# An attention and feed-forward layer on one core: new due times for slot zero's statistics, additions and low parts, and for slot one's first scores

## The chip, the cores and the metric

The kernel runs on one core of a Trainium2 chip. The metric is the device time of one execution in microseconds (us): the median of the runs, less is better.

## What is computed

There are 8 slots (batches) of x and ctx, each [512, 2048] in fp32. The reference, cut to what matters:

```python
xn = layernorm(x)                                # over the 2048 columns of each row
t, p, g = Wt @ ctx, Wp @ xn, Wg @ ctx            # [512, 512] weights
att = sum over each group of 64 rows of p * g    # one number per group
y  = Wz (per group) @ (att * t)
yn = groupnorm(y) * gn_w + gn_b
x  = x + yn + ctx
h  = layernorm(x)[:, perm] as 16 heads of 128 columns
x  = x + unpermute(down[head] @ gelu(up[head] @ h))
```

## The kernel before, in words

**The algebra.** Since att is a sum of products of p and g, the kernel never forms p or g. It forms the scores S = x ctx^T over the 2048 columns (16 blocks dt of 128), corrects S with the mean and the deviation of x's rows, multiplies it by Wp (stage v_mm) and reduces it against Wg (v_att). Wz Wt is folded into one matrix at the start (fold_mm), and Y = (Wz Wt) ctx is computed in four quarters q of 512 columns (y_mm). Then come the group statistics (g_mean, g_var_mm, g_var_a, g_root, g_var_b), the sum (x1_piece), the second layernorm, a transposed store to a scratch in HBM, and the units of the feed-forward part, which gather 128 rows by an index, run up, gelu, down and scatter the result.

**High and low parts.** TensorE takes fp32 operands rounded to its fp32r format. For full accuracy each operand is split: ScalarE makes the high part (s_hi line 976, y_hi line 982), VectorE the low part by subtraction (s_lo line 1084, y_lo line 1090). TensorE runs three products: high x high (s_hh line 874, for four banks c1), then low x high and high x low (s_mm lines 879 and 880). For Y a group of twelve matmuls (line 892 x8, then line 896 x4) makes one tile ot of one quarter; the last four need the low part.

**The order of work.** There is one plan, `plan()`. Each stage gets a due time by `put(t, stage, ...)`, in units of about 2.72 us (the time of one block). The stages are sorted by due time, and each engine then runs its own stages in that one order, first in, first out. A stage waits on semaphores for its inputs and for its buffers (`take` and `give`), and an engine's later stages wait behind it. So a due time does nothing but set the order on the engines. Slot zero starts at base 0, its y0 is 16, v0 is 32 and f0 is 36; slot one starts at base 36.

**The stages around the change, in slot zero.**
- VectorE: bn_x (statistics of x tile ct, quarter q; 16 pieces, line 1069), aggr_x (line 1076), s_lo, y_lo, add_c (X += ctx, 16 pieces, line 1096, on VectorE for slot zero alone), sum_c (lines 1107 to 1112), bn_y (line 1132), s_fix (line 1120), s_evl (line 1126), v_att (line 1151), g_mean, g_var_a (lines 1171 and 1173), g_var_b.
- ScalarE: s_hi, y_hi, row_c (row sums of ctx, four pieces a quarter, line 991), y_ev (empties two banks of Y, line 998), s_evh (line 1006). In the order: y_hi(0,1), row_c(0,1,0..3), y_ev(0,0,0), row_c(0,2,0..3), y_ev(0,0,1), y_hi(0,2), row_c(0,3,0..3), y_ev(0,1,0).
- GpSimd (POOL): the splitting of the feed-forward weights, head by head: load_raw (two transfers of 256 KB), w_hi (line 1278), w_lo (line 1283), keep_w (a store of 1,024 KB, line 1288); then root_x, g_root. The stage w_hi(11) waits for s_lo(0,15) beside its data.
- SyncE: all other loads. ctx quarters c(0,q) and score blocks s(i,j) share three buffers RAW. c(0,1) takes the one of s(0,6), c(0,2) that of s(0,7), and so waits for s_lo(0,15); c(0,3) takes the one of c(0,0), and so waits for y_lo(0,0), row_c(0,0,*) and add_c(0,0,*).
- TensorE: y_mm(0,q,ot) waits for y_hi(0,q), for y_lo(0,q) ahead of its last four matmuls, and for y_ev of the quarter before for its bank. s_hh(1,0,c1) waits for v_att(0,c1), which reads the same bank. The waits of the first block and of the variance matmul, in the code:

```python
                if dt == 0:
                    for t in free["sb", i, c1]:
                        pe.wait_ge(*t)
...
            elif stage == "g_var_mm":
                i = a[0]
                pe.wait_ge(*at["gst", i, "sum"])
```

DMAs issued by GpSimd go to the queue that the profile calls q0 software_dynamic, those of SyncE to q1 hardware_dynamic.

## Time and profile before

| | |
|---|---|
| median of 3 runs | 1518.26 us |
| the runs | 1518.26, 1518.87, 1514.97 us |
| span of the profiled execution | 1516.6 us (the page gives no other time of it) |
| TensorE busy | 1496.1 us, 99% |
| VectorE, ScalarE, GpSimd busy | 1192.4, 1065.8, 962.8 us |
| mean granted TensorE clock | 0.999 |
| DMA | 374.76 MB, mean 247 GB/s |

The span goes from the first to the last instruction of one profiled execution; the times of the runs are taken without a profile. A matmul's end is modelled in the profile, so a busy share of TensorE says that it had matmuls in flight, not that none was late. Starts are exact, and some matmul records are missing. Matmuls of one group stand merged in the timeline with their count. Times in the views are us from the start of the span.

### The profile page before, as it was taken

The page shows a single profiled execution, that of the slowest core. Times are in us where ns is not written, and L with a number is a line of the kernel's source. Part 1 is how long each engine was busy: PE and PEld are TensorE (multiplying, and loading weights), DVE is VectorE, ACT ScalarE, POOL GpSimd, SP SyncE. Part 2 cuts the span into 40 slices and gives each one's busy share as a digit, 9 for nine tenths or more (in the row PEclk, how much of TensorE's full clock was granted, in tenths as well). Part 3 has the DMA queues.
Part 4 walks back from the last instruction along what each step waited for, and adds up shares of the span by engine and source line. Part 5 has one row for each costly group of instructions (what it writes and reads, how often), then busy time and mean ns, then how long its engine had stood idle before and what let it go on. Part 6 is the DMA issues. An engine that isn't in the chain of part 4 may idle for free.

```text
span 1516.6 us, 19144 instructions
## 1 busy us (share of the span) xinstructions
PE 1496.1 (99%) x6592; PEld 1233.7 (81%) x6592; DVE 1192.4 (79%) x1514; ACT 1065.8 (70%) x1321; POOL 962.8 (63%) x765
## 2 busy tenths in 40 slices
PE   8999999998999999999999999999999999999998
PEld 7878888887888888888888888888888888777886
DVE  4989868875788767887678877888778876889876
ACT  4636757844878568784687847878378773899876
POOL 1673686297862668626784357834579355898887
PEclk9999999999999999999999999999999999999999
DMA  9998788786677936778376784767747776768886
GB/s 327 330 379 332 229 301 298 269 265 204 202 264 266 276 118 221 246 262 278 119 237 248 246 260 133 261 237 250 231 146 275 249 237 204 236 197 257 289 285 221
DMA packets 166865, 374.76 MB, mean 247 GB/s; under 512 B 14960, under 2 KB 80496, under 8 KB 158576
## 3 DMA queue, kind: packets, MB, share of 16 engines
q1 hardware_dynamic: 141424, 281.25, 56.3%
q0 software_dynamic: 25344, 92.29, 17.3%
q8 instruction: 52, 0.85, 0.2%
q14 instruction: 45, 0.37, 0.1%
HBM read 287.45 MB, written 86.03 MB: 246 GB/s over the span
## 4 chain that ended last, share of the span: by engine, by line
PE 80%; DVE 4%; POOL 4%; DMA 4%; ACT 3%; issue 3%; SPq 0%; POOLq 0%; ACTq 0%; DVEq 0%
PE PP L892 13%; PE PP L938 12%; PE PP L953 12%; PE PP L896 6%; PE PP L941 6%; PE PP L957 6%; PE PP L879 6%; PE PP L880 6%; PE PP L874 6%; PE PP L909 4%; PE PP L913 2%; POOL out L1346 1%; POOL FB L1338 1%; POOL FB L1341 1%; ACT Z L1031 1%
## 5 line engine op out<-in xcount | busy, mean ns | idle before, releaser
L938 PE MATMUL PP<-GG,WW 128*128 128x512 f32 x1008 | 270.5, 390 | 4.4 <-issue 4.4
L1046 ACT ACTIVATE PP<-PP 128x1024 f32<-128x1024 f32 x256 | 262.0, 1024 | 0.0
L1249 DVE TENSOR_TENSOR R<-PP,R 128x1024 fp32r<-128x1024 f32 x175 | 213.6, 1220 | 52.5 <-ACT PP L1046 50.6
L892 PE MATMUL PP<-R,WC 128*128 128x512 f32 x1024 | 253.1, 389 | 0.7 <-ACT Z L998 0.7
L1330 POOL TENSOR_TENSOR X<-X,RAW 128x512 f32<-128x512 f32 x112 | 189.2, 1725 | 96.4 <-DVE bn L1069 71.6
L1045 ACT ACTIVATE R<-PP 128x1024 fp32r<-128x1024 f32 x175 | 180.1, 1029 | 87.5 <-PE PP L941 86.5
L938 PEld LDWEIGHTS PP<-GG,WW 128*128 128x128 f32 x1008 | 189.6, 188 | 44.4 <-issue 4.8
L892 PEld LDWEIGHTS PP<-R,WC 128*128 128x128 f32 x1024 | 192.1, 188 | 41.0 <-ACT Z L998 1.1
L1084 DVE TENSOR_TENSOR R<-RAW,R 128x1024 fp32r<-128x1024 f32 x128 | 184.1, 1445 | 49.8 <-ACT R L976 49.8
L1346 POOL DMA_INDIRECT out<-FB,perm_sb x128 | 153.4, 1198 | 82.0 <-DVE FB L1255 64.1
L1323 POOL DMA_INDIRECT FB<-xg_scratch,perm_sb x128 | 127.7, 997 | 115.1 <-DMA xg_scratch<-FB 74.4
L879 PE MATMUL PP<-R 128*128 128x512 f32 x512 | 200.5, 392 | 0.1
L880 PE MATMUL PP<-R 128*128 128x512 f32 x512 | 200.2, 391 | 0.0
L1338 POOL TENSOR_TENSOR FB<-FB,SMM 128x512 f32<-128x512 f32 x128 | 167.3, 1307 | 49.8 <-DVE GG L1244 38.3
L1341 POOL TENSOR_TENSOR FB<-FB,SMM 128x512 f32<-128x512 f32 x128 | 186.6, 1458 | 10.1
L953 PE MATMUL PP<-R,WW 128*128 128x512 f32 x688 | 185.5, 391 | 2.0 <-DMA WW<-w_scratch 2.0
L976 ACT CAST R<-RAW 128x1024 fp32r<-128x1024 f32 x128 | 132.1, 1044 | 73.2 <-PE PP L880 47.2
L941 PE MATMUL PP<-GG,WW 128*128 128x512 f32 x504 | 155.9, 391 | 0.9 <-DVE GG L1244 0.9
L874 PE MATMUL PP<-R 128*128 128x512 f32 x512 | 150.1, 392 | 5.4 <-ACT R L976 5.2
L953 PEld LDWEIGHTS PP<-R,WW 128*128 128x128 f32 x688 | 128.0, 188 | 28.6 <-issue 2.7
L1255 DVE TENSOR_TENSOR FB<-PP,FB 128x512 f32<-128x512 f32 x128 | 87.7, 685 | 64.9 <-PE PP L957 63.0
L896 PE MATMUL PP<-R,WC 128*128 128x512 f32 x512 | 137.1, 390 | 1.2 <-DVE R L1090 1.1
(122 smaller groups left out, 2582.5 us busy)
## 6 DMA issues: line engine op xcount, KB each, us to landing
WW<-w_scratch SPq DMA_DIRECT2D x148, 512.0 KB
X<-in_x SPq DMA_DIRECT2D x32, 1024.0 KB, 6.0
RAW<-in_cx SPq DMA_DIRECT2D x32, 1024.0 KB
RAW<-in_xT SPq DMA_DIRECT2D x63, 512.0 KB
RAW<-in_cT SPq DMA_DIRECT2D x63, 512.0 KB
xg_scratch<-FB SPq DMA_DIRECT2D x104, 256.0 KB
w_scratch<-WW POOLq DMA_DIRECT2D x16, 1024.0 KB, 6.8
HX<-wp_scratch SPq DMA_DIRECT2D x7, 1024.0 KB, 8.2
```

What stands on the lines that cost most here:

```text
L874: eng.matmul(s_bank(c1), hi[:, 0, part(c1)], hi[:, 1, :], start=(dt == 0), stop=False)
L879: eng.matmul(s_bank(c1), lo[:, 0, part(c1)], hi[:, 1, :], start=False, stop=False)
L880: eng.matmul(s_bank(c1), hi[:, 0, part(c1)], lo[:, 1, :], start=False, stop=(dt == ND - 1)).then_inc(S["smm"], 1)
L892: eng.matmul(PP[2 + ot // 2][:, ot % 2, :], WC[:, l, ct, part(ot)], u[:, ct, :], start=(l == 0 and ct == 0), stop=False)
L896: t = eng.matmul(PP[2 + ot // 2][:, ot % 2, :], WC[:, 0, ct, part(ot)], u[:, 4 + ct, :], start=False, stop=(ct == NT - 1))
L938: eng.matmul(pp[:, e, :], wt[:, l, part(2 * p + e)], g[:, 0, :], start=(l == 0), stop=False)
L941: t = eng.matmul(pp[:, e, :], wt[:, 0, part(2 * p + e)], g[:, 1, :], start=False, stop=True)
L953: eng.matmul(PP[1][:, f % 2, :], wt[:, 2 + l, part(2 * p + e)], hi[:, e, :], start=(p == 0 and e == 0 and l == 0), stop=False)
L1046: eng.activation(pp[:], pp[:], ACT.Gelu).then_inc(S["gelu"], 1)
L1249: eng.tensor_tensor(h_tile(f, p, 1), PP[slot["up", f, p]][:], f32(h_tile(f, p, 0)), ALU.subtract).then_inc(S["hlo"], 1)
L1330: eng.tensor_tensor(X[:, ct, cols(q)], X[:, ct, cols(q)], RAW[slot["c", i, q]][:, ct, :], ALU.add).then_inc(S["xc"], 1)
L1341: eng.tensor_tensor(rows, rows, SM[b % 2][:, 1], ALU.add).then_inc(S["radd"], 1)
```

## The change

The change gives new due times to some stages; no stage is added or removed, and no stage's code is touched. In slot zero: the statistics of x tiles 1 to 3 (bn_x) are due 0.85 later, which puts them behind s_lo(0,15) and partly behind y_lo(0,0); y_lo(0,1) is due at 15.45, not 16.6; the additions add_c have a table of their own, which puts those of quarters two and three behind y_lo(0,2). g_var_mm, g_var_a and g_root are due one block later. In slot one the first score matmul of the fourth bank, s_hh(1,0,3), is due at 36.35, not 36.24.

Sorted by due time, the orders of ScalarE, GpSimd and SyncE stay as they were. On TensorE s_hh(1,0,3) comes behind s_mm(1,0,0), and g_var_mm(0) behind the four s_hh(1,3,*) rather than behind those of block 2. VectorE's order from s_lo(0,14) on, before and after:

```
before: s_lo 14, bn_x(1,0..3), s_lo 15, bn_x(2,0), y_lo 0, bn_x(2,1..3), add_c(0,0), bn_x(3,0..1),
        add_c(0,1), bn_x(3,2..3), add_c(0,2..3), y_lo 1, add_c(1,0..2), aggr_x, add_c(1,3), bn_y(0,0..1),
        add_c(2,0..2), y_lo 2, bn_y(0,2), add_c(2,3), bn_y(0,3), add_c(3,0), sum_c, ...
after:  s_lo 14, s_lo 15, bn_x(1,0..2), y_lo 0, bn_x(1,3), bn_x(2,0..3), add_c(0,0..1), bn_x(3,0), y_lo 1,
        bn_x(3,1), add_c(0,2), bn_x(3,2..3), add_c(0,3), add_c(1,0..2), aggr_x, add_c(1,3), bn_y(0,0..1),
        y_lo 2, add_c(2,0), bn_y(0,2), add_c(2,1), bn_y(0,3), add_c(2,2), sum_c, add_c(2,3), ...
```

```diff
--- before.py
+++ after.py
@@ -602,12 +602,12 @@
             put(t + 0.2, s_lo, i, dt)
             for c1 in range(NT):
                 whole = i < 2 or dt > 3
-                put(s0 + (dt + 0.08 * c1 if whole else S_EARLY[c1 // 2][dt][c1 % 2]), s_hh, i, dt, c1)
+                put(s0 + (0.35 if (i, dt, c1) == (1, 0, NT - 1) else dt + 0.08 * c1 if whole else S_EARLY[c1 // 2][dt][c1 % 2]), s_hh, i, dt, c1)
                 put(s0 + (dt + 0.34 + 0.16 * c1 if whole else S_EARLY[c1 // 2][dt][c1 % 2]), s_mm, i, dt, c1)
         for q in range(NQ):
             for ct in range(NT):
                 t = s0 + 6 + 2.1 * ct + 0.4 * q + (1.9 if ct == 3 else 0)
-                t = 10.4 + 1.4 * ct + 0.22 * q if first else s0 + 11 + 2.1 * ct + 0.5 * q if i == 1 else t
+                t = 10.4 + 1.4 * ct + 0.22 * q + (0.85 if ct else 0) if first else s0 + 11 + 2.1 * ct + 0.5 * q if i == 1 else t
                 put(t, bn_x, i, ct, q)
         if first:
             for ct in range(NT):
@@ -619,11 +619,11 @@
         put(y0 + (12.4 if 0 < i < 3 else 4.2), load_wg, i)
         for q, t in enumerate((y0 - 3, y0 + 0.4, y0 + 4.3, y0 + 8.3)):
             put(t, y_hi, i, q)
-            put(t + 0.2, y_lo, i, q)
+            put(y0 - 0.55 if first and q == 1 else t + 0.2, y_lo, i, q)
         for q, t in enumerate((y0 - 1, y0 + 1.2, y0 + 2.6, y0 + 4.6)):
             for ct in range(NT):
                 put(t + 0.25 * ct + late, row_c, i, q, ct)
-                put(y0 - 1.5 + 2.4 * q + 0.5 * ct + 2 * late, add_c, i, q, ct)
+                put(y0 + (-1.2, 0.9, 4.6, 6.4)[q] + 0.5 * ct if first else y0 - 1.5 + 2.4 * q + 0.5 * ct + 2 * late, add_c, i, q, ct)
         put(y0 + 5.8 + late, sum_c, i)
         put(y0 + 5.9 + late, store_sum, i)
         put(y0 + 7.6 + late, spread_sum, i)
@@ -648,9 +648,9 @@
         put(v0 + 3.4, aggr_y, i)
         put(f0 + 1.2, g_mean_mm, i)
         put(f0 + 1.25, g_mean, i)
-        put(f0 + 2.3, g_var_mm, i)
-        put(f0 + 2.35, g_var_a, i)
-        put(f0 + 2.4, g_root, i)
+        put(f0 + (3.3 if first else 2.3), g_var_mm, i)
+        put(f0 + (3.35 if first else 2.35), g_var_a, i)
+        put(f0 + (3.4 if first else 2.4), g_root, i)
         put(f0 + (3.9 if first else 5.25), g_var_b, i)
```

## Rows read from the trace of the kernel before

**Rows 1.** the page: busy time, share of the span and instructions of each engine

```profile
PE 1496.1 (99%) x6592; PEld 1233.7 (81%) x6592; DVE 1192.4 (79%) x1514; ACT 1065.8 (70%) x1321; POOL 962.8 (63%) x765
```

**Rows 2.** TensorE's waits, whole span; us in total, times, longest

```profile
PE PP L938 <- issue: 4.4, 1, 4.4
```

**Rows 3.** TensorE's timeline, 52 to 82 us: start, us, engine, line, operation

```profile
52.24 1.07 PE L874 MATMUL PP<-R 128*128 128x512 f32 x4
...
53.70 0.39 PE L880 MATMUL PP<-R 128*128 128x512 f32 x1
...
66.19 1.98 PE L892 MATMUL PP<-R,WC 128*128 128x512 f32 x8
...
69.30 1.99 PE L892 MATMUL PP<-R,WC 128*128 128x512 f32 x8
...
72.03 1.98 PE L892 MATMUL PP<-R,WC 128*128 128x512 f32 x8
...
77.47 1.98 PE L892 MATMUL PP<-R,WC 128*128 128x512 f32 x8
...
81.56 1.98 PE L892 MATMUL PP<-R,WC 128*128 128x512 f32 x8
```

**Rows 4.** TensorE's timeline, 100 to 120 us

```profile
100.60 1.15 PE L909 MATMUL PP<-R,HX 128*128 128x512 f32 x4
...
111.57 0.84 PE L874 MATMUL PP<-R 128*128 128x512 f32 x3
...
112.92 0.39 PE L879 MATMUL PP<-R 128*128 128x512 f32 x1
...
117.72 1.07 PE L874 MATMUL PP<-R 128*128 128x512 f32 x4
...
119.34 0.48 PE L879 MATMUL PP<-R 128*128 128x512 f32 x1
```

**Rows 5.** VectorE's timeline, 47 to 91 us

```profile
49.72 2.47 DVE L1069 BATCH_NORM_STATS2 bn<-X 128x6 f32<-128x512 f32 x4
...
53.83 2.73 DVE L1090 TENSOR_TENSOR R<-RAW,R 128x2048 fp32r<-128x2048 f32 x1
...
65.93 2.28 DVE L1090 TENSOR_TENSOR R<-RAW,R 128x2048 fp32r<-128x2048 f32 x1
...
75.98 4.48 DVE L1090 TENSOR_TENSOR R<-RAW,R 128x2048 fp32r<-128x2048 f32 x1
```

**Rows 6.** GpSimd's timeline, 47 to 82 us; in brackets idle time before, and releaser

```profile
53.37 1.04 POOL L1278 CAST WW<-FB 128x1024 fp32r<-128x1024 f32 x1 [3.55 <-DVE R L1084]
...
59.12 0.56 POOL L1288 DMA_DIRECT2D w_scratch<-WW  x1 [0.30 <-POOL WW L1283]
...
75.60 2.72 POOL L1283 TENSOR_TENSOR WW<-FB,WW 128x1024 fp32r<-128x1024 f32 x1
```

**Rows 7.** DMA queues from 52 to 57, then 57 to 60 us: packets, MB, share

```profile
q0 software_dynamic: 278, 1.50, 73.0%
q1 hardware_dynamic: 275, 0.55, 29.3%
...
q1 hardware_dynamic: 516, 1.02, 94.0%
q0 software_dynamic: 19, 0.02, 3.1%
```

**Rows 8.** ScalarE's timeline, 47 to 100 us

```profile
47.49 2.00 ACT L976 CAST R<-RAW 128x1024 fp32r<-128x1024 f32 x2 [5.77 <-DMA RAW<-in_cT]
...
60.03 1.91 ACT L982 CAST R<-RAW 128x2048 fp32r<-128x2048 f32 x1 [5.24 <-DMA RAW<-in_cx]
...
64.74 1.00 ACT L998 COPY Z<-PP 128x1024 f32<-128x1024 f32 x1
...
71.35 0.63 ACT L991 ACTIVATE FB<-RAW 128x512 f32<-128x512 f32 x1
...
99.77 0.69 ACT L1006 ACTIVATE R<-PP,rs 128x512 fp32r<-128x512 f32 x1 [1.22 <-DVE PP L1120]
```

## The prediction

> **What bounds the kernel now.** I read the page first: TensorE is busy for 99% of the span [rows 1], so time moves only where TensorE waits, and every other engine matters by what it makes TensorE wait for. The list of TensorE's waits comes next. Its second entry, 4.4 us, is one wait near 351 us for the gathered rows of slot two [rows 2], which the diff does not name; the rest are small. The list undercounts, because a matmul's recorded end is modelled. So I read the starts in the timeline: twelve matmuls take 2.73 us from start to start, 0.227 us each (69.30 to 72.03), and a longer step is a loss [rows 3].
>
> Five losses lie beside instructions that the diff moves:
> - last scores of slot zero: 52.24 to 53.70 is 1.46 us for five matmuls (the fifth has no row here), due 1.14: **0.32 us**;
> - first Y group of quarter one: 66.19 to 69.30 is 3.11 against 2.73: **0.39 us**;
> - first Y group of quarter two: 77.47 to 81.56 is 4.09 against 2.73: **1.37 us**. These three are in [rows 3];
> - first scores of slot one: 111.57 to 112.92 is 1.35 for four, due 0.91: **0.44 us**;
> - the matmul for the group variance: 117.72 to 119.34 is 1.62; 0.91 for the four before it and about 0.2 for the two tiny ones leave **0.5 us**. These two are in [rows 4].
> Together 3.0 us, 0.2% of the time. That is all the change can win directly.
>
> **The change part by part.** Sorting the stages by their due times, old and new, shows that the order changes on VectorE and TensorE alone; the ScalarE, GpSimd and SyncE orders are the same, and nothing is added or removed.
>
> (a) s_lo(0,15) goes ahead of the four statistics of x tile 1. It ran behind bn_x x4, which began at 49.72 [rows 5]. Its source was ready: the two s_hi from 47.49 took 2.00 us, to 49.5 [rows 8]. So it now runs 49.7 to 50.9. TensorE needs it at 53.15. Gain 0.32. Price of the moved statistics: nothing, they have until aggr_x near 70.
>
> (b) y_lo(0,0) then starts at 50.9 + 3 x 0.6 = 52.7 instead of 53.83, bn_x(0,1,3) behind it. It meets GpSimd, see (c). In the trace, when GpSimd's subtraction was there first (75.60 to 78.32), y_lo took 4.48 us from 75.98 instead of 2.28, so it waited 2.2 us, to 78.2, and then ran [rows 5, 6]. GpSimd's subtraction now runs 52.1 to 54.8 at worst, y_lo(0,0) ends by 57.0; TensorE, 0.32 earlier, wants it at 55.0 + 1.8 = 56.8. Cost 0 to 0.2; I take 0, and 0.2 stays in the range.
>
> (c) What hangs on s_lo(0,15) beside TensorE: GpSimd's w_hi(11) waits for it, and in the trace it was released by it at 53.37 after 3.55 us idle [rows 6]. It now starts at 51.0, 2.4 us earlier, and its subtraction is ahead of y_lo(0,0), not behind it. So keep_w(11) and load_raw(13), issued from 59.12 on [rows 6], are issued from about 55. That is 1.57 MB (1,024 KB and two of 256 KB) on the software queue, 4 us earlier. SyncE's load_c(0,2) waits for s_lo(0,15) too and is issued 2.4 us earlier, behind load_c(0,1) on the same queue, so it gives nothing.
>
> What that traffic meets: between 52 and 57 us the software queue moved 1.50 MB and the hardware queue 0.55 MB, in 278 and 275 packets; between 57 and 60 us, with the software queue empty, the hardware queue moved 1.02 MB in 516 packets [rows 7]. So sharing costs the hardware queue two thirds of its pace (55 packets per us against 172, a factor 3.1), with the engines full in both. The context quarter c(0,1) is what it carries, and it landed at 60.0, when ScalarE, idle for 5.24 us, took it [rows 8]. In the changed kernel the software queue is not empty from 57 on: 1.57 MB at 0.30 MB per us is 5.2 us, to 62.2. If the last part of c(0,1) needs all of the 3.0 us from 57 to 60 to itself, 5.2 us shared do 1.7 us of it, and it lands at 63.5. If only 2 of the 3 us are its own, 57 + 2 x 3.1 = 63.2. Bounds: 60.0 (it is done before the traffic reaches its engines) and 65.2 (it is held for all 5.2 us). I take 63.2, by the shared pace, the only row that has both queues busy.
> The Trainium skill, "DMA: Bandwidth & Descriptors", section on queues, rings and completion order, says that each DMA engine takes its queues in turn, packet by packet. By the near-equal packet counts the trace agrees; were it instead shared by bytes, c(0,1) would land near 61.5 and the sum below would be -1.7.
>
> Who waits for c(0,1): ScalarE's order is y_hi(0,1), four row sums, then y_ev(0,0,0), which started at 64.74 and ended at 65.74 [rows 8]. That frees the bank for y_mm(0,1,0), which started at 66.19 on time [rows 3]. So TensorE can start quarter one no sooner than landing + 5.7. With TensorE 0.32 early at 65.87, any landing after 60.2 costs one for one; this slack was 0.45 us before. At 63.2 quarter one starts at 68.9, **2.7 us later** than before.
>
> (d) y_lo(0,1) goes ahead of five statistics and two additions, and starts when y_hi(0,1) ends (landing + 1.95) instead of at 65.93 [rows 5]. It is needed 1.8 us after the quarter's start, 7.5 after the landing, and ends 4.2 to 6.5 after it. Gain 0.39, kept.
>
> (e) y_lo(0,2) goes ahead of add_c(0,2,0..2). In the trace it began at 75.98, with GpSimd's subtraction from 75.60 in its way [rows 5, 6]. Now it starts at about 72.9 (landing 60.0) or 75.5 (63.2, where y_hi(0,2) and the statistics bring it) and is needed at 79.0 or 81.6. Gain 1.37, kept unless it is blocked for more than 3.8 us; the longest block seen is 2.2.
>
> (f) The additions pushed back give their buffers later: c(0,3) takes the buffer of c(0,0), which add_c(0,0,3) gives up at 65.93, just before y_lo(0,1) [rows 5]. Now that addition ends 4.2 + 3.1 = 7.3 us after c(0,1) lands, 67.3 or 70.5. c(0,3) was in ScalarE's hands at 71.35, 5.4 us after its issue [rows 8], so it comes at 72.7 or 75.9; row sums and y_ev(0,1,0) end 3.9 later, 76.6 or 79.8. TensorE wants that bank at 76.8 or 79.8. Cost 0, but with no slack.
>
> (g) First scores of slot one: the fourth bank's matmul goes behind two that wait for nothing (0.45 us), more than the wait: gain 0.44. (h) The variance matmul goes one block (2.7 us) later: gain 0.5, and x1's chain behind it starts up to 0.6 us later, hidden because nothing of TensorE's waits on slot zero's x1 pieces in this stretch; its list of waits names none.
>
> **Sum.** +2.7 - 0.39 - 1.37 - 0.44 - 0.5 = 0.0 us; for a landing L after 60.2, the net is L - 63.2. The span stays 1516.6. The page gives the span of the profiled execution alone; the median of the runs is 1.7 above it, and their own spread is 1514.97 to 1518.87. I forecast 1518.2. About 0.3% (4.6 us) is what a measurement of this kernel can tell from no change.
>
> **Rivals.**
> 1. The direct gains come through: the traffic does not slow c(0,1). For it: most of c(0,1) may be home by 57. Against: rows 7 show full engines. -3.0, so 1515.2. Chance 0.27.
> 2. TensorE is early and is stopped at v_mm. s_evh's last piece ended at 100.46 and v_mm began at 100.60 [rows 4, 8]: 0.14 us of slack on a chain that comes from sum_c through two transfers. sum_c should come 4 us earlier; if those transfers do not, 2.1 of the 3.0 us go: -1.0, so 1517.3. Chance 0.08.
> 3. Slower: c(0,1) is held for the whole burst (65.2, +2.0) and c(0,3) in its turn by the burst of keep_w(12), now issued after root_x at about 77. With no slack in (f), every us beyond 5.4 counts; the same hold costs 3.2. +5.2, so 1523.4. It decides from the point where c(0,1) lands after 63.2 or c(0,3) takes over 5.4 us. Chance 0.08.
> 4. Faster by more: the 4.4 us wait at 351 us [rows 2] hangs on a chain of stores, transposes and gathers; a shifted start may shorten it. -3 to -7, about 1513. Chance 0.10.
> 5. It does nothing that shows, each wait being taken over by its neighbour: 1518.3. Chance 0.05.
> The forecast's own chance is 0.42, its own range -1.7 to +1.5.
>
> The range, 1512.8 to 1521.8, holds the forecast, rivals 1, 2 and 5 and half of 3 and 4. Faster by over 0.3%: 0.13 (rival 4 and the edge of 1); slower: 0.05; within: 0.82.
>
> **What the changed profile would show.** Right: s_lo(0,15) before 51; w_hi(11) at 51; keep_w(11) near 55; y_hi(0,1) starting near 63 with ScalarE idle for 8 us before it; TensorE's quarter one starting near 69 behind y_ev; no step over 2.8 us at the first groups of quarters one and two; none at the first scores or the variance matmul. Wrong: y_hi(0,1) still at 60 (rival 1); a gap ahead of the first v_mm (rival 2); y_hi or row sums of c(0,3) after 76 with a gap at quarter two (rival 3); another size of the gap near 351 (rival 4).

## The result, and the profile after

The changed kernel is slower. Its median is 1525.02 us (1520.4 to 1528.72, 16 runs) against 1518.57 us (1514.81 to 1524.65, 16 runs) for the kernel before on the same chip: a ratio of 1.0038, 95% interval 1.0027 to 1.0049. That is 6.45 us more, outside the forecast range. The profiled execution took 1524.99 us with a span of 1523.2 us.

The page of the changed kernel, its span and its busy times (beside [rows 1]):

```profile
span 1523.2 us, 19144 instructions
PE 1497.9 (98%) x6592; PEld 1232.9 (81%) x6592; DVE 1194.8 (78%) x1514; ACT 1065.4 (70%) x1321; POOL 959.2 (63%) x765
```

TensorE's waits in the changed kernel (engine, line waited for: us in total, times, longest):

```profile
PE PP L892 <- ACT Z L998: 8.4, 3, 4.5
...
PE PP L909 <- ACT R L1006: 1.7, 1, 1.7
PE PP L938 <- issue: 0.6, 1, 0.6
```

The wait of 4.4 us near 351 us [rows 2] is down to 0.6. In its place TensorE waits three times, 8.4 us in all, at the first eight matmuls of a Y group (L892) for ScalarE to empty their bank (L998), near 76, 180 and 345 us; before, that was one wait of 0.7 us. TensorE's timeline shows where (start, us, engine, line, operation, count; idle time and its releaser in brackets):

```profile
65.20 1.98 PE L892 MATMUL PP<-R,WC 128*128 128x512 f32 x8
...
67.92 1.98 PE L892 MATMUL PP<-R,WC 128*128 128x512 f32 x8
...
75.18 1.07 PE L896 MATMUL PP<-R,WC 128*128 128x512 f32 x4
78.11 2.11 PE L892 MATMUL PP<-R,WC 128*128 128x512 f32 x8 [1.86 <-ACT Z L998]
...
99.09 1.07 PE L896 MATMUL PP<-R,WC 128*128 128x512 f32 x4
101.87 1.16 PE L909 MATMUL PP<-R,HX 128*128 128x512 f32 x4 [1.72 <-ACT R L1006]
...
113.77 0.39 PE L880 MATMUL PP<-R 128*128 128x512 f32 x1
114.64 0.50 PE L874 MATMUL PP<-R 128*128 128x512 f32 x1 [0.49 <-DVE am L1151]
...
178.51 1.07 PE L896 MATMUL PP<-R,WC 128*128 128x512 f32 x4
184.03 3.78 PE L892 MATMUL PP<-R,WC 128*128 128x512 f32 x8 [4.45 <-ACT Z L998]
187.61 1.74 PE L896 MATMUL PP<-R,WC 128*128 128x512 f32 x4
189.19 2.01 PE L892 MATMUL PP<-R,WC 128*128 128x512 f32 x8
```

By the pitch of 0.227 us, the changed kernel loses 2.0 us at 78.11, 1.9 at 101.87 and 0.6 at 114.64. The first Y group of quarter one (65.20 to 67.92, 2.72 us) has lost its wait, as forecast [rows 3]. **The large loss lies in slot one, ahead of quarter two of Y.** The four matmuls from 178.51 are due to be followed at 179.42; the next starts at 184.03, 4.6 us late. The eight after it take 3.58 us from start to start (184.03 to 187.61) in place of 1.81, and the four after these 1.58 in place of 0.91. That is another 2.4 us, 7.0 together. In that second part the granted clock is at its lower level. Stretches of the changed kernel (us, busy time of each engine with instructions, PEclk, DMA share, GB/s):

```profile
180.00:184.00 4.00, 0.00 (x0) 0.00 (x0) 2.39 (x4) 2.36 (x6) 3.40 (x4) 0.77 0.78 214
184.00:188.00 4.00, 3.97 (x9) 3.14 (x10) 3.88 (x7) 3.97 (x6) 3.98 (x5) 0.50 0.86 255
188.00:192.00 4.00, 4.00 (x17) 3.21 (x16) 4.00 (x5) 0.06 (x1) 4.00 (x3) 0.87 0.85 193
```

TensorE stands idle, and its granted clock falls from full speed to 0.50 (2.4 to 1.2 GHz), and the first matmuls behind the wait run at half speed.

One matmul of the group mean (L923) marks each slot. It moves from 115.44 to 117.05 in slot zero (+1.6), from 215.12 to 223.23 in slot one (+8.1), from 364.09 to 368.42 in slot two (+4.3, since the wait near 351 gives some back in this execution), and stays at +4.3 up to the last slot, 1291.36 to 1295.71. The profiled spans differ by 6.6; the other 2.3 us come behind that mark, where this stretch varies from 224.5 to 228.9 us over the profiles of this case. That remainder has no cause here.

What ScalarE's bank waited for is told by the chain of waits of the changed kernel, read from 50 to 200 us (start, us, what; "issue" is time in which the profile shows no wait):

```profile
74.10 14.15 DMA FB<-in_down
88.31 1.05 POOL WW L1278
...
115.30 8.57 DMA FB<-in_down
123.93 1.75 POOL WW L1278
...
129.38 1.06 POOL rs L1315
...
132.62 1.20 DVE Z L1206
...
154.72 8.07 ACT Z L1031 x4
...
172.58 1.31 POOL X L1330
...
173.97 7.61 DMA RAW<-in_cx
...
183.08 0.91 ACT Z L998
```

It reads: the loads of GpSimd's weight heads (in_down) are late, so g_root (L1315), which stands behind the heads on GpSimd, is late, so slot zero's x1 (L1206) is late; behind it come the second layernorm, the statistics and additions of slot one, the load of c(1,3) into the buffer they free, its row sums (L991) and the emptied bank (L998). The same stations in the kernel before, on VectorE, GpSimd, ScalarE and TensorE:

```profile
84.13 1.04 POOL L1278 CAST WW<-FB 128x1024 fp32r<-128x1024 f32 x1 [3.65 <-DMA FB<-in_down]
...
124.68 1.87 POOL L1315 TENSOR_TENSOR rs<-ve,half 128x4 f32<-128x4 f32 x1
...
128.66 1.28 DVE L1206 SCALAR_TENSOR_TENSOR Z<-Z,sm,X 128x1024 f32<-128x1024 f32 x1
...
175.31 0.64 ACT L991 ACTIVATE FB<-RAW 128x512 f32<-128x512 f32 x1 [2.38 <-DMA RAW<-in_cx]
176.70 0.99 ACT L998 COPY Z<-PP 128x1024 f32<-128x1024 f32 x1
...
178.40 1.98 PE L892 MATMUL PP<-R,WC 128*128 128x512 f32 x8
```

There the bank is emptied at 177.7 and taken at 178.40. So the chain already had only 0.7 us of slack before the change, behind no wait in any list. After it, the first x1 piece is 4.0 us later and c(1,3) 6.3.

### The profile page after: what moved, and what is told of

The parts are those of the page before. It is cut to its first block, busy times and chain, and to the rows that moved or that the text cites. A ratio compares the mean times of both kernels' runs of the same rounds, so it can differ in the third digit from the quotient of the medians.

```text
span 1523.2 us, 19144 instructions
## 1 busy us (share of the span) xinstructions
PE 1497.9 (98%) x6592; PEld 1232.9 (81%) x6592; DVE 1194.8 (78%) x1514; ACT 1065.4 (70%) x1321; POOL 959.2 (63%) x765
## 4 chain that ended last, share of the span: by engine, by line
PE 72%; POOL 9%; DMA 7%; issue 5%; ACT 4%; DVE 2%; SPq 0%; POOLq 0%; ACTq 0%; DVEq 0%
PE PP L953 12%; PE PP L938 12%; PE PP L892 11%; PE PP L941 6%; PE PP L957 6%; PE PP L896 5%; PE PP L874 5%; PE PP L879 5%; PE PP L880 5%; PE PP L909 3%; DMA FB<-in_down 3%; POOL FB L1338 2%; POOL out L1346 2%; PE PP L913 2%; POOL FB L1341 2%
## 5 line engine op out<-in xcount | busy, mean ns | idle before, releaser
L892 PE MATMUL PP<-R,WC 128*128 128x512 f32 x1024 | 255.0, 391 | 8.4 <-ACT Z L998 8.4
L892 PEld LDWEIGHTS PP<-R,WC 128*128 128x128 f32 x1024 | 193.1, 189 | 49.8 <-ACT Z L998 9.6
L1341 POOL TENSOR_TENSOR FB<-FB,SMM 128x512 f32<-128x512 f32 x128 | 189.9, 1484 | 10.1
L1255 DVE TENSOR_TENSOR FB<-PP,FB 128x512 f32<-128x512 f32 x128 | 87.6, 684 | 62.5 <-PE PP L957 62.5
```

Of the source, the lines that this page charges most:

```text
L892: eng.matmul(PP[2 + ot // 2][:, ot % 2, :], WC[:, l, ct, part(ot)], u[:, ct, :], start=(l == 0 and ct == 0), stop=False)
L1341: eng.tensor_tensor(rows, rows, SM[b % 2][:, 1], ALU.add).then_inc(S["radd"], 1)
```

## The experiments

A ratio is that to the kernel before, run beside the variants on the same chip; its medians were 1518.91, 1518.53, 1519.71, 1518.34 and 1519.63 us beside the five groups. Each variant has 12 timed runs; of the 35 runs of the kernel before beside group C one took 3913.82 us, which does not move the median. A view shows one execution, and not always a typical one: c1, c4, d1, e1 and f2 were profiled in executions 4.7 to 9.0 us above their own medians. In c1, c4, f1 and f2 TensorE starts 8.3 to 9.9 us late near 360 us, in the other profiles of this case 0.8 to 4.6 (the kernel before 4.6, the changed one 0.8). So the medians tell what a variant costs, and the views, up to the mark of slot one, where it loses. "Lost near 184" is the late start of TensorE at quarter two of slot one and what the matmuls behind it lose.

**Group A: the change taken apart.** a1 is the changed kernel with g_root (due at 39.4) put ahead of the last weight head on GpSimd; the other three are the kernel before with some lines of the shown diff.

```diff
 a1 (on the changed kernel)
         put(t, load_raw, h)
+        t += 3.1 if h == 3 else 0
         put(t + 3.3, w_hi, h)
 a2: the lines of s_hh(1,0,3), g_var_mm, g_var_a, g_root alone
 a3: the line of bn_x alone
 a4: the lines of y_lo(0,1) and add_c alone
```

> The changed kernel with one more edit: GpSimd does g_root of slot zero before it splits head 3 (w_hi, w_lo, keep_w of head 3 are due after it), not after. Theory (the loss is made on GpSimd: its weight pipeline is late, g_root stands behind it, and x1, the statistics of slot one, c(1,3) and y_ev of slot one follow): g_root ends near 125 instead of 130.4, the stalls of TensorE in quarter three of slot one (178 to 189 us in the changed kernel, 7 us in all) fall to under 1.5 us, and the time falls by 3 to 7 us, to 1518 to 1522. Rival (the loss is made in slot zero by the later c(0,3) and the sum chain, and slot one's stall has its own cause, the loads of slot one): the stall stays at 5 us or more and the time within 1.5 us of the changed kernel's 1525.

> The kernel before with the last two parts of the change alone: s_hh(1,0,3) behind s_mm(1,0,0), and g_var_mm, g_var_a, g_root of slot zero one block later. Both theories: 0.4 to 1.0 us are won at 111 to 120 us; g_root stays behind the store of head 3 on GpSimd, so nothing behind it moves by more than 0.7 us. Time 1517.6, within 1.5 us of before. Rival (the later variance matmul delays x1 and through it slot one): a stall over 2 us at quarter three of slot one, and 2 to 5 us slower.

> The kernel before with only bn_x of tiles 1 to 3 due 0.85 later: s_lo(0,15) and y_lo(0,0) come forward, y_lo(0,1) and the additions keep their due times. Theory: GpSimd's head 11 starts 2.4 us early, its store and the loads of head 13 meet c(0,2), and y_lo(0,0) waits for GpSimd's subtraction; c(0,3) is issued at 66 to 67 as before, the burst behind it does not meet the loads of head 14. Slot one has no long stall; time within 2 us of before, 1517 to 1520. Rival (the early head 11 is what makes GpSimd's pipeline late): w_hi of head 14 starts after 87, g_root ends after 129, 3 to 7 us slower.

> The kernel before with only y_lo(0,1) ahead and the new table for add_c of slot zero; the statistics keep their due times. Theory: add_c(0,0,3) ends later, so c(0,3) is issued 2 to 3 us later than 66.1, and with it the loads and stores of 3 MB that stand behind it on SyncE; they meet keep_w(12) and the loads of head 14, w_hi of head 14 starts after 87 instead of 84.1, g_root ends 3 to 5 us later, slot one stalls: 3 to 7 us slower, 1521.5 to 1525.5. Rival (the early head 11 does it): w_hi of head 14 within 1 us of before, time within 2 us of before or up to 2 us faster, since y_lo(0,2) is in time.

| | median, us | ratio (95%) | first x1 piece | lost near 184 |
|---|---|---|---|---|
| a1 | 1519.93 | 1.0013 (0.9992 to 1.0034) | 129.24 | 0.9 |
| a2 | 1518.55 | 1.0009 (0.9991 to 1.0027) | 128.54 | 1.3 |
| a3 | 1518.33 | 1.0002 (0.9988 to 1.0016) | 128.79 | none |
| a4 | 1522.14 | 1.0015 (1.0004 to 1.0025) | 130.80 | 2.6 |

a1: with g_root ahead of the last head most of the loss is gone, though the wait ahead of v_mm (1.76 us) is as long as in the changed kernel. So the chain over g_root counts, and that wait does not decide. The last head itself now runs beside VectorE's small operations behind it (one of 128x4 takes 2.25 us in place of 0.16), and x1 is still 0.6 us late. a2: TensorE's two parts do nothing that shows. The slot-zero mark is 1.0 us early (114.43) and the slot-one mark only 0.3 (214.85): the gain is swallowed where slot one is gated. a3: the statistics alone do nothing that shows either; TensorE stops 1.05 us at 65.40, since y_hi(0,1) came at 60.70. That is my step (c) in small. a4: the lines of VectorE's low parts and additions make part of the loss (1.0015 against the changed kernel's 1.0038, intervals that do not meet). But here c(0,3) was issued at 66.1, the same as in the kernel before. So my first theory, that the late c(0,3) is the root of the loss, does not hold for a4.

**Group B: one suspected wait taken away each.**

```diff
 c1 (on the changed kernel: y_lo(0,1) behind the last add_c of quarter zero)
-            put(y0 - 0.55 if first and q == 1 else t + 0.2, y_lo, i, q)
+            put(y0 + 0.35 if first and q == 1 else t + 0.2, y_lo, i, q)
 c3 (on the changed kernel: head 11 behind y_lo(0,0))
                 if h == 11:
                     pool.wait_ge(*at["slo", 0, ND - 1])
+                    pool.wait_ge(*at["ylo", 0, 0])
 c4 (on the changed kernel: the two 1 MB stores of Wp's parts behind slot one's third score load)
-    put(21.5, keep_wp)
+    put(31.0, keep_wp)
 d1 (on the kernel before: the lines of a2, the line of a1, y_lo(0,2) early, gathers of slot two ahead of head 7)
-            put(t + 0.2, y_lo, i, q)
+            put(y0 + 3.25 if first and q == 2 else t + 0.2, y_lo, i, q)
+            hold = 1.0 if h == 7 else 0
```

> The changed kernel with y_lo(0,1) behind add_c(0,0,3) again, as before the change, all else as changed. Theory A (c(0,3) issued 2.9 us late brings the 3 MB behind it on SyncE into the way of keep_w(12) and the loads of head 14): c(0,3) is issued near 66.5 instead of 69.0, the stall at quarter two (75 to 78 us) goes, w_hi of head 14 starts near 84.5 instead of 88.3, g_root comes 2 to 4 us earlier, time 1519 to 1522. Theory B (any shift of GpSimd's stream against SyncE's does it): the stall at quarter two goes, but w_hi of head 14 stays after 86.5 and the time above 1522.5.

c1 measured 1524.14 us, 1.0023 (1.0004 to 1.0042). Here c(0,3) is issued at 65.4 and the loss at quarter two is gone, yet most of the time stays. The first x1 piece is at 129.70, but c(1,3) took 7.8 us from issue to ScalarE, and TensorE lost 7.0 us near 184 and started 8.3 us late near 360; this profiled execution took 1530.58 us. The late c(0,3) is worth about its own 2.0 us: the ratio is 1.0023 against 1.0038, with intervals that overlap.

> The changed kernel, where GpSimd's w_hi(11) waits for y_lo(0,0) too (a later release, near 54 instead of 50.3, about where it was before the change). If the early head 11 (its store and the loads of head 13 meeting c(0,2), and y_lo(0,0) blocked by GpSimd's subtraction) is a cause: y_lo(0,0) takes 2.3 us instead of 4.0, c(0,2) lands near 62.5 instead of 65.0, and the time falls by 1 to 3 us. If it is not: y_lo(0,0) is short, c(0,2) early, but c(0,3) still late and the time within 1 us of 1525.

c3 measured 1523.93 us, 1.0026 (1.0005 to 1.0047). Held back, GpSimd no longer blocks y_lo(0,0) (2.27 us in place of 4.03), and head 11 runs at 54.10. Head 14 comes at 87.93 all the same, the first x1 piece at 132.40. The early head 11, the whole of my step (c), is not the cause.

> The changed kernel with SyncE's two stores of Wp's parts (2 MB, issued at 70 to 71 us) moved behind load_s(1,2), to about 91. Theory A and B both put the loss on what the hardware queue carries while keep_w(12) and the loads of head 14 are under way (73 to 88 us): w_hi of head 14 then starts by 84 instead of 88.3, g_root 2 to 4 us earlier, the stalls in slot one fall by as much, time 1519 to 1523; part of it may come back when the stores meet later heads. Rival (the loads of head 14 wait for something else than bandwidth, their own queue): w_hi of head 14 stays at 88, time within 1.5 us of 1525.

c4 measured 1522.46 us, 1.0008 (0.9989 to 1.0028). With 2 MB of other traffic taken away, head 14 comes at 82.14 in place of 88.31: the stores had taken its DMA time. But the stores collide with later heads (the last two at 115.41 and 121.83), and x1 is still at 131.66. By the ratio part of the loss is gone; the execution profiled took 1527.13 us, 4.7 above the median, and does not show where.

> A version drawn from the findings, from the kernel before: the two parts at 111 to 120 us (s_hh(1,0,3), variance matmul), y_lo(0,2) ahead of add_c(0,2,0..2) alone, g_root ahead of the splitting of head 3 on GpSimd, and in slot two the gathers ahead of the splitting of head 7. Nothing on SyncE or GpSimd before 80 us moves. Expected: 0.9 us from the first, 1.2 from the second, g_root 4 us earlier (no stall at quarter three of slot one), and 2 to 3 us of the 4.4 us wait near 351. In all 3 to 6 us faster than before, 1513 to 1516. It would fail if the gathers have nothing to fetch before 350 anyway (the stores of x's last quarter land near 348): then 1 to 3 us faster.

d1 measured 1518.45 us, 0.9982 (0.9963 to 1.0001). An attempt at a better kernel, it does not show the 3 to 6 us expected. In the profiled execution it keeps the gains of slot zero (mark 113.69 in place of 115.44) and loses 6.7 us near 184, where c(1,3) took 7.1 us (mark 219.52 in place of 215.12). But that execution took 1527.46 us, 9.0 above the median, so it does not show what a typical one loses.

**Group C: the last head behind x1.** The line of a1 and one wait more, so that the last head blocks neither g_root nor VectorE's small operations.

```diff
 e1 (on the changed kernel), e2 (on the kernel before), e3 (on the kernel before, with the lines of a2 and d1's y_lo(0,2)):
+        t += 3.1 if h == 3 else 0
...
+                if h == 3:
+                    pool.wait_ge(*at["x1", 0, NT - 1, 1])
 e4: the changed kernel again, no edit
```

> The changed kernel with g_root of slot zero ahead of head 3 on GpSimd, and w_hi(3) waiting for the last x1 piece of slot zero, so that GpSimd does nothing beside g_root, g_var_b and the x1 pieces. Theory (the time is set by the chain g_root, x1, second layernorm, statistics and additions of slot one, load of c(1,3), y_ev, which ended 0.7 us before TensorE wanted it in the kernel before): the first x1 piece starts near 127 instead of 132.5 (129.2 with head 3 merely behind g_root), c(1,3) is issued 41.4 us after it, near 168.5, TensorE does not wait for y_ev at quarter one of slot one, and the time is 1515 to 1519. Rival (slot one's stall is set by how long the load of c(1,3) takes, 5.0 to 7.8 us in the profiles so far, not by when it is issued): a stall over 1.5 us there, time 1520 or more.

> The same edit of GpSimd on the kernel before, nothing else. Theory: the chain ended before TensorE's need there, so that chain coming 1 to 3 us earlier gives TensorE nothing at slot one; only the 4.4 us wait of slot two, if it hangs on the same chain, may shrink. Time 1515.5 to 1519, the same as before within 0.2%. Rival (that chain already costs the kernel before some us that the profile does not show): 2 to 5 us faster.

> The kernel before with the parts of the change that moved nothing on GpSimd or SyncE (s_hh(1,0,3), the variance matmul, y_lo(0,2) ahead of add_c(0,2,0..2)) and GpSimd's edit of the two kernels above. Theory: TensorE is 2.1 us early at Y of slot one, and the chain is early too, so this time the gain is kept: first x1 piece near 126, no stall for y_ev in slot one, 1.5 to 3 us faster than before, 1515.5 to 1517. Rival (the gain is taken by the next chain, at slot two's wait near 351): slot one without a stall, slot two's wait longer by as much, time within 1 us of before.

> The changed kernel once more, for a second profile beside the same chip's kernel before. Theory: the delays on GpSimd are set by the order of the queues and come again: first x1 piece at 132 to 133, c(0,3) issued near 69, a stall of 4 us or more for y_ev in slot one, time 1524 to 1526. If the late landing of c(1,3) (7.6 us after its issue, 5.0 in the kernel before) is chance, it will land sooner here and that stall be near 2.5 us.

| | median, us | ratio (95%) | first x1 piece | c(1,3): issued, at ScalarE | lost near 184 |
|---|---|---|---|---|---|
| e1 | 1517.26 | 0.9987 (0.9965 to 1.0009) | 129.37 | 172.66, 179.30 | 1.2 |
| e2 | 1518.80 | 0.9990 (0.9969 to 1.0011) | 127.03 | 170.79, 175.82 | none |
| e3 | 1516.35 | 0.9971 (0.9950 to 0.9992) | 127.86 | 170.96, 176.49 | none |
| e4 | 1526.87 | 1.0034 (1.0009 to 1.0060) | 133.65 | 175.13, 182.58 | 6.3 |

e1: the changed kernel without the last head in its way is as fast as the kernel before, with every direct loss of slot zero still in it (2.24 us ahead of v_mm, 1.09 at quarter two). It is at the time expected; x1 and c(1,3) came later than I wrote (the profiled execution took 1523.31 us, 6.0 above the median). e2: for the kernel before the same edit is worth nothing that shows; it had its 0.7 us of slack. e3 is faster than the kernel before by 0.29% (0.08% to 0.50%), and nothing is lost near 184. That TensorE's two parts and the early y_lo(0,2) come through once the gate of slot one has slack fits this; no run separates them. e4: the changed kernel repeats its result and its picture (head 14 at 88.36, the same 7.45 us for c(1,3)).

**Group D: g_root alone, and the two halves of a4.**

```diff
 f3 (on the kernel before)
             elif stage == "g_root":
                 i = a[0]
                 pool.wait_ge(*at["gst", i, "vaa"])
+                if i == 0:
+                    pool.wait_ge(*at["shi", 1, 8])
 f1: the kernel before with the line of y_lo(0,1) alone
 f2: the kernel before with the line of add_c alone
 f4: the changed kernel without the lines of a2
```

> The kernel before with one wait more and nothing moved: slot zero's g_root waits for the high part of block 8 of slot one, which ends at 128.03 us in the trace of before. g_root so starts at 128.1 in place of 124.26, and everything up to 124 us stays as it was. Theory one (slot one is gated by the chain g_root, x1, second layernorm, statistics of slot one, c(1,3), and that alone makes the changed kernel slower): first x1 piece at 132.3 to 132.7, c(1,3) issued near 174, TensorE loses 3 to 7 us near 180 to 190, median +3 to +6.5, that is 1521.6 to 1525. Rival (the loss is made ahead of 124 us, by the transfers and the additions, and the x1 chain only looks late beside it): median within 1 us of the kernel before and no wait over 1 us near 184.

f3 measured 1524.89 us (1518.27 to 1531.69), 1.0030 (1.0011 to 1.0049). Its g_root on GpSimd, and TensorE's timeline:

```profile
128.18 0.22 POOL L1315 TENSOR_SCALAR ve<-sm 128x4 f32<-128x4 f32 x1 [2.76 <-ACT R L976]
```

```profile
177.54 1.07 PE L896 MATMUL PP<-R,WC 128*128 128x512 f32 x4
181.96 3.78 PE L892 MATMUL PP<-R,WC 128*128 128x512 f32 x8 [3.35 <-ACT Z L998]
185.53 1.91 PE L896 MATMUL PP<-R,WC 128*128 128x512 f32 x4
```

Nothing was moved, only g_root made to start at 128.18 in place of 124.26. The first x1 piece came at 131.66, c(1,3) was issued at 173.11 and reached ScalarE at 179.53, and TensorE lost 6.5 us from 177.54 on (3.5 waiting, 3.0 at the lower clock). The median is the changed kernel's, 6.5 us above the kernel before; the ratio gives 4.6 us (1.7 to 7.4). **A late g_root by itself makes a loss of this size at this place.**

> The kernel before with y_lo(0,1) alone moved: it goes ahead of the last two additions of quarter zero, and every other stage stays. It is one half of the run that had y_lo(0,1) and the table of additions together and cost 3.6 us. Theory one (the early y_lo(0,1) makes those two additions late, GpSimd's weight heads shift with them, and g_root with these): w_hi of head 14 near 85 us, first x1 piece near 130.8, median about 1521.5 to 1522.5. Theory two (the table of additions does it): first x1 piece at 128.5 to 129.0, as before, and a median within 1 us of the kernel before.

f1 measured 1526.07 us, 1.0043 (1.0024 to 1.0062), first x1 piece 131.75.

> The kernel before with the table of additions alone: VectorE's additions of quarters two and three stand behind y_lo(0,2) and the statistics of y, and two statistics of x go ahead of the first additions. It is the other half of the run with both. Theory one (the early y_lo(0,1) is guilty): first x1 piece at 128.5 to 129.0 and a median within 1 us of the kernel before, with the wait at the first group of quarter two gone. Theory two (the table is guilty, since each heavy GpSimd operation meets another VectorE instruction): w_hi of head 14 later than 84.5, first x1 piece near 130.8, median about 1521.5 to 1522.5. If neither half does it alone and both together do, it is the meeting of the two engines and no single moved stage.

f2 measured 1524.27 us, 1.0026 (1.0006 to 1.0047), first x1 piece 131.71. Neither theory of mine had this: each half alone does the harm, and no less than both together in a4 (1.0015). What the two share is VectorE's last low part, y_lo(0,3): it ends at 87.3 (f1) and 87.2 (f2), in the kernel before at 90.7 and in f3 at 90.5. It frees a buffer for SyncE's score loads 3 us sooner.

> The changed kernel without its two parts on TensorE: the first score matmul of the fourth bank of slot one and the variance matmul with its chain are back at their old places. Theory one (GpSimd's weight heads hold g_root, so a variance that comes one block later costs nothing of its own): g_root still ends after 130, first x1 piece at 132 to 133, median 1524 to 1526.5. Rival (the later variance matmul adds its up to one block of 2.7 us to the chain of x1): first x1 piece at 130 to 131.5, median about 1522 to 1523.

f4 measured 1524.09 us, 1.0037 (1.0016 to 1.0057), first x1 piece 132.12: theory one. The later variance matmul adds nothing that shows; GpSimd's heads hold g_root longer than it does.

**Group E: why the heads are late.** DMA queues from 90 to 100 us (packets, MB, share of 16 engines), first the kernel before, then the changed kernel, then g1:

```profile
q1 hardware_dynamic: 531, 1.69, 48.4%
q0 software_dynamic: 343, 1.89, 48.4%
```

```profile
q1 hardware_dynamic: 771, 2.54, 64.3%
q0 software_dynamic: 288, 1.51, 37.5%
```

```profile
q0 software_dynamic: 404, 2.39, 62.1%
q1 hardware_dynamic: 350, 1.16, 38.3%
```

The software queue carries GpSimd's weight heads. In the changed kernel it gets 1.51 MB in place of 1.89, because SyncE's queue moves 2.54 MB in place of 1.69: the third pair of score loads of slot one goes at 90.41 and 90.79, in the kernel before at 91.87 and 93.33. f1 and f2 look the same (SyncE 2.55 and 2.34 MB); a3 and f3, whose heads are on time, look like the kernel before (1.64 and 1.60). a4 and c1, whose third pair goes at 87.8 and 88.5, partly ahead of this window, lie between (2.14 and 2.03) with head 0 at 101.0 in both. How much sooner the pair goes because of the freed buffer is not shown: in the kernel before it goes right behind a load that took 1.73 us to issue, in the changed kernel 0.42. In a1 and e3 the traffic is as in the slow ones (2.43 and 2.68), but there g_root does not stand behind the last head. g1 is f2, and g2 the changed kernel, with that one transfer held back:

```diff
             elif stage == "load_s":
...
+                if (i, j) == (1, 2):
+                    sp.wait_ge(*at["sevh", 0, 3])
                 eng.dma_start(RAW[k][:, 0:2, :], xT[i, rows, :]
```

> The table of additions alone on the kernel before, with one wait more on SyncE: the third pair of score loads of slot one, 1 MB, waits for the last s_evh of slot zero (about 101.6 us) in place of going at about 90. Seen so far: between 90 and 100 us SyncE's queue moved 2.34 to 2.55 MB in the three slow versions looked at and 1.60 to 1.69 MB in the three where g_root's chain is on time, and GpSimd's own loads got 1.20 to 1.51 MB in place of 1.71 to 1.93. Theory one (VectorE is done earlier with the last low parts, so buffers come free and SyncE's score loads go 2 us earlier, and they take the DMA engines from the weight heads that g_root stands behind): SyncE's queue moves under 1.7 MB between 90 and 100, w_hi of head 0 comes near 99 in place of 102.1, g_root starts near 125 in place of 128.5, first x1 piece 128.5 to 129.3, median 1518 to 1520. Rival (the heads are late for another reason, such as VectorE blocking GpSimd): w_hi of head 0 after 101, first x1 piece after 130.5, median 1523 to 1525.

g1 measured 1518.71 us (1515.33 to 1525.61), 0.9999 (0.9980 to 1.0018). The GpSimd and VectorE rows of g1:

```profile
99.48 1.04 POOL L1278 CAST WW<-FB 128x1024 fp32r<-128x1024 f32 x1 [1.47 <-DMA FB<-in_down]
...
124.61 1.05 POOL L1315 TENSOR_TENSOR rs<-ve,half 128x4 f32<-128x4 f32 x1
```

```profile
127.78 1.28 DVE L1206 SCALAR_TENSOR_TENSOR Z<-Z,sm,X 128x1024 f32<-128x1024 f32 x1
```

Head 0 is at 99.48 in place of f2's 102.07, g_root at 124.61 in place of 128.55, and TensorE loses nothing near 184. One transfer of 1 MB sent 8 us later (97.98) takes g_root back, and with it the difference between the medians of f2 (1524.27) and g1, 5.6 us; the ratios to the kernel before are 1.0026 and 0.9999, with intervals that overlap. It is not all that the early y_lo(0,3) does. In f2 that low part (84.96 to 87.24) meets GpSimd's cast of head 14:

```profile
85.28 2.87 POOL L1278 CAST WW<-FB 128x1024 fp32r<-128x1024 f32 x1 [4.38 <-DMA FB<-in_down]
```

It takes 2.87 us in place of 1.04, and the load of head 0 is issued at 92.01 in place of 89.36. Then it needs 10.1 us in f2, 8.9 in the kernel before and 7.9 in g1, where the cast is as long (2.97) and the load goes at 91.57. So holding the transfer was enough, but it made good a delay that came from the cast too.

> The changed kernel with the same wait on SyncE. Here head 14's weights are late too (88.3), which comes ahead of 90 us from the time when no transfer ran (65 to 70 us), so theory one wants only a part back: w_hi of head 0 near 100 in place of 103.8, first x1 piece 129.5 to 131, TensorE's loss near 184 under 3 us in place of 7, median 1520 to 1522.5. Rival: first x1 piece after 132 and the median still 1524 to 1526.5.

g2 measured 1520.85 us, 1.0002 (0.9986 to 1.0019). TensorE lost 2.4 us near 184 in place of 7.0, and c(1,3) took 5.5 us. Head 0 (102.15) and the first x1 piece (131.57, outside the 129.5 to 131 expected) came back only in part: x1 is 1.0 us earlier than in the changed kernel, c(1,3) is issued 1.0 us earlier and reaches ScalarE 3.1 us earlier. So most of the time came back with a faster c(1,3), which no run explains. What is left is head 14, at 88.90, ahead of the transfer that was moved. In the changed kernel the load of head 0 goes 3.9 us later than before (93.22 against 89.36) because head 14 is late, and takes 1.7 us longer. The windows of 65 to 70 us show what it lacks, first in the kernel before, then in the changed one (last three columns: PEclk, DMA share, GB/s):

```profile
65.00:70.00 5.00, 4.89 (x22) 3.70 (x22) 5.00 (x7) 4.91 (x11) 0.00 (x0) 1.00 0.58 176
```

```profile
65.00:70.00 5.00, 5.00 (x24) 4.14 (x23) 5.00 (x9) 4.85 (x10) 0.00 (x0) 1.00 0.01 2
```

For 5 us the DMA engines move nothing in the changed kernel: SyncE's queue stands at c(0,3) until 69.0, and behind it wait Wg and the Wp stores, while GpSimd's next load waits for aggr_x on VectorE. That this gap makes head 14 late agrees with c4; it was not tried by itself.

## Why the prediction was wrong

**What held.** The five direct losses were read rightly, and four of them went much as worked out. (a) s_lo(0,14) and s_lo(0,15) ran from 47.84 to 50.20, and GpSimd's head 11 from 50.27, 3.1 us earlier. (b) y_lo(0,0) met GpSimd's subtraction and took 4.03 us; TensorE lost 0.5 there, over the 0.2 kept in the range. (d) and (e): the waits for y_lo(0,1) and y_lo(0,2) are gone. (h): the matmuls around the variance, at 122.96 in the changed kernel, start on time. VectorE's rows of the changed kernel:

```profile
51.91 4.03 DVE L1090 TENSOR_TENSOR R<-RAW,R 128x2048 fp32r<-128x2048 f32 x1
...
58.84 4.25 DVE L1096 TENSOR_TENSOR X<-X,RAW 128x512 f32<-128x512 f32 x2
...
63.61 2.27 DVE L1090 TENSOR_TENSOR R<-RAW,R 128x2048 fp32r<-128x2048 f32 x1
```

**What failed, by its steps.** The step that decided is the last half of (h): "hidden because nothing of TensorE's waits on slot zero's x1 pieces in this stretch; its list of waits names none". TensorE does wait on them, 50 us later and through the stations of the chain above, and no list showed it because the chain was just in time, with 0.7 us of slack. The step had x1 up to 0.6 us late at no cost; x1 came 4.0 us late, and TensorE lost 7.0 us behind it. f3 prices such a delay: g_root 3.9 us later, the median 6.5 us higher. The 0.6 us of (h) are not where it came from (f4): the sum had nothing for the weight heads, which hold g_root. It failed together with a thing left out. I costed the queues where the change moved an instruction, between 47 and 82 us. I did not ask what SyncE would issue once VectorE was done sooner. In f2 the answer is score loads at 90 us beside the weight heads ahead of g_root: g1 took their effect away. In the changed kernel they are one part; the other is head 14, late since the gap of 65 to 70 us, whose cause was not tried.

**Terms that were mis-sized.** (c), the largest term (+2.7): c(0,1) was to land at 63.2 and ScalarE took it at 58.51, earlier than before, so the term was 0; rival 1 was right about that transfer. Its sum has a slip too: it shares the engines until 63.2, though the burst ends at 62.2, which gives 62.5; and the 61.5 for sharing by bytes has no working. The factor 3.1 rests on near-equal packet counts in one window; with both queues loaded from 90 to 100 us they are 343 to 531 and 288 to 771. With c(0,1) at 60.70 in a3 TensorE did stop 1.05 us there, so the slack was as small as the step said. In the changed kernel ScalarE had to wait 0.84 us for c(0,2), until 65.05, which cost TensorE nothing. ScalarE's rows of the changed kernel:

```profile
58.51 1.91 ACT L982 CAST R<-RAW 128x2048 fp32r<-128x2048 f32 x1 [4.37 <-DMA RAW<-in_cx]
...
65.05 0.63 ACT L991 ACTIVATE FB<-RAW 128x512 f32<-128x512 f32 x1 [0.84 <-DMA RAW<-in_cx]
...
74.17 0.63 ACT L991 ACTIVATE FB<-RAW 128x512 f32<-128x512 f32 x1 [3.40 <-DMA RAW<-in_cx]
...
77.06 1.91 ACT L998 COPY Z<-PP 128x1024 f32<-128x1024 f32 x2
```

(f), "Cost 0, but with no slack": it cost 2.0 us. Two small additions that took 4.25 us between them from 58.84 (four take 2.47 where GpSimd is quiet) and the low part ahead of them pushed back the last addition; c(0,3) was issued 10.4 us after c(0,1) came, in place of the 7.3 counted, 2.9 us later than before, and was in ScalarE's hands at 74.17. (g): the gain of 0.44 did not come. TensorE was done with v_mm at 112.86, and VectorE began the reduction that frees the fourth bank 1.0 us later, at 113.84 (in the kernel before 0.2 us later, 111.77 behind 111.57), straight behind a copy that took 1.10 us in place of 0.44; the loss is 0.6. Rival 2's gate, s_evh ahead of v_mm, was real and cost 1.9 us in place of its 0.14 us of slack. It came as that rival says: sum_c's store went 2.0 us earlier (81.19), but the load behind it at 88.14 in place of 88.29, and s_fix (L1120) started at 95.78, before at 94.50.

**Rival 3** ended on the right side with nearly the right time (1523.4 against 1525.0), but by another mechanism: of its two holds the first did not happen and the second was worth 2.0 us. It would be wrong to call it confirmed. **Rival 4** pointed at a real thing: the wait at 351 us changed, but what it gave back (4.3 - 8.1 = -3.8 us from slot one to two) was less than slot one had lost. That it follows the start of slot two is not shown: with slot one's mark at 223.23, 223.47 and 221.16 (changed kernel, e4, f2) TensorE was 0.8, 2.4 and 8.6 us late there.

The Trainium skill, "SBUF — State Buffer", section on the two separate sides, calls the port pair of VectorE and GpSimd an exclusive lock that the loser waits for during the whole instruction. The trace agrees: y_lo(0,0) took 4.03 us beside GpSimd's subtraction and 2.27 without it (c3). The rule moved single instructions by 2 us. c3 took this one away and the time stayed.

**Left open.** c(1,3), 1 MB, reached ScalarE 5.0 to 5.6 us after its issue in the kernel before, a1 to a4, c3, c4, e2, e3, f1, f4, g1 and g2, and 6.4 to 7.8 us in the changed kernel, e4, c1, d1, e1, f2 and f3. In the two profiles of the changed kernel it is alike (7.63 and 7.45), so it may belong to the order of transfers; every other kernel has one profile, and those of c1, d1, e1 and f2 are 6 to 9 us above their medians, so chance is not ruled out. Which transfer it meets was not tried. It is why 4 us at the first x1 piece become 6.3 at ScalarE.

## What to carry to other kernels

A list of waits shows where slack is already below zero, not where it is 0.7 us: before calling an edit hidden, follow what it feeds forward to the next place where TensorE takes a buffer, over as many stages as it takes, and write down the slack found there. Ask of every instruction that ends sooner which buffer it frees and which queue then sends what: here a low part that ended 3 us sooner on VectorE let 1 MB go early and met a cast on GpSimd, and the loads on which the next slot's start hung came late. Hold back transfers that nothing needs yet, and put a small operation that a long chain hangs on (g_root) ahead of bulk work on its engine.

## What the runs showed of the hardware that I had not expected

- A wait of TensorE of 4.6 us costs more than itself: the granted clock went to 0.50 and twelve matmuls took 5.16 us in place of 2.72. In f1, after 9.9 us of waiting near 360 us, it stayed at 0.50 from 362 to 370.
- GpSimd's queue moved less where SyncE's moved more, with the DMA engines full in both cases: from 90 to 100 us (DMA share 0.97 and 1.02) at 359 GB/s in all (before) and 406 (after), the software queue had 1.89 and 1.51 MB.
- Freeing DMA time in one place moved the lateness rather than taking it away (c4: head 14 6.2 us earlier, the last head 2.1 us earlier, x1 0.9 us earlier).
